# First attention's projection of the tile behind, placed later in the step on every engine, and a second place for the normalised output

## The reference

```python
x = _layernorm(x + _L0_attn_ref(x, Wq, Wk, Wv, proj_w, proj_b))        # 16 heads of 64, causal
x = _layernorm(x + _L0_xattn_ref(x, ctx_1024, ctx_1024, mask, ...))    # 16 heads of 16, context of 77 rows
x = _layernorm(x + _L0_ffn_ref(x, Wr, W1, b1, W2, b2, fw1, ...))       # 8 experts, top 2, capacity, fallback
```

## Time and profile before

| | value |
|---|---|
| Median of three runs | 1508.05 us |
| Time of the profiled execution | 1509.21 us |
| Its span | 1507.5 us |
| PE busy | 1301.3 us (86%) |
| PEld busy | 1079.2 us (72%) |
| DVE busy | 1083.8 us (72%) |
| ACT busy | 924.1 us (61%) |
| POOL busy | 721.1 us (48%) |
| Mean granted clock of PE | 0.956 |
| First and last copy of `o_t` (L782) | 78.8 and 981.3 us, 32 of them |

### The profile page before, as it was taken

How to read it: one execution, slowest core, us unless ns; L and a number is a source line. 1 busy time by engine, 2 the same in 40 slices (tenths; PEclk the granted TensorE clock), 3 DMA queues, 4 the chain that set the end, 5 groups by cost and what they waited for, 6 DMA issues and landing times. The chain is left out here.

```text
span 1507.5 us, 47409 instructions
## 1 busy us (share of the span) xinstructions
PE 1301.3 (86%) x16821; PEld 1079.2 (72%) x16821; DVE 1083.8 (72%) x3112; ACT 924.1 (61%) x2287; POOL 721.1 (48%) x970
## 2 busy tenths in 40 slices
PE   3589999999999999999999999864899999999930
PEld 2478778778878877887887887632688888888820
DVE  4678888888888888888888888748455555555537
ACT  3566777778777777777877766514344444444426
POOL 3144564674565566566556644420243344343326
PEclk9899999999999999999999999995899999999975
DMA  9657767667657667676676664019333363333235
GB/s 222 145 138 161 171 169 160 137 145 175 142 140 184 132 140 190 130 150 155 154 154 142 153 105 90 24 61 421 125 75 76 75 163 93 80 75 77 70 139 206
DMA packets 293216, 208.95 MB, mean 139 GB/s; under 512 B 218782, under 2 KB 250654, under 8 KB 290560
## 3 DMA queue, kind: packets, MB, share of 16 engines
q1 hardware_dynamic: 281952, 184.01, 51.0%
q0 software_dynamic: 6816, 17.71, 4.1%
q10 hardware_dynamic: 4224, 4.19, 0.8%
HBM read 93.79 MB, written 65.93 MB: 106 GB/s over the span
## 5 line engine op out<-in xcount | busy, mean ns | idle before, releaser
L1729 PE MATMUL ps_e<-xt,wres 128*128 128x128 f16 x3408 | 343.5, 220 | 5.2 <-DMA xt<-xg 4.2
L1729 PEld LDWEIGHTS ps_e<-xt,wres 128*128 x3408 | 285.8, 99 | 77.1 <-issue 5.9
L1793 ACT ACTIVATE act_g<-ps_e,b 128x128 f32<-128x128 f32 x568 | 162.4, 369 | 208.1 <-PE ps_e L1729 206.3
L1736 PE MATMUL ps_e<-wres,g_hi 128*128 x568 | 214.5, 379 | 0.8 <-DVE g_lo L1816 0.8
L743 ACT ACTIVATE probs<-st_k,nmax 128x128 f32<-128x128 f32 (+1 forms) x512 | 199.9, 448 | 1.9 <-DVE nmax L964 1.6
L964 DVE CUSTOM_DVE_ANT_0 st_k<-ps,causal 128x128 f32<-128x128 f32 (+1 forms) x512 | 160.6, 351 | 38.0 <-PE ps L444 37.9
L1696 POOL DMA_INDIRECT z_scr<-e_y,dst_i x71 | 82.9, 1168 | 212.6 <-DVE e_y L1807 212.6
L750 ACT ACTIVATE pt_hi<-ps 128x384 f16<-128x384 f32 x256 | 125.2, 489 | 56.0 <-PE ps L452 27.7
L1738 PE MATMUL ps_e<-wres,g_lo 128*128 x568 | 154.8, 273 | 0.0
L452 PE MATMUL ps<-ident,probs 128*128 128x128 f32 x768 | 130.5, 279 | 24.4 <-ACT probs L743 19.3
L969 DVE TENSOR_TENSOR pt_lo<-ps,pt_hi 128x384 f16<-128x384 f32 x256 | 141.4, 552 | 6.0 <-ACT pt_hi L750 2.6
(11 more groups left out here) (281 smaller groups left out, 4044.9 us busy)
## 6 DMA issues: line engine op xcount, KB each, us to landing
k_pair<-k_pair SPq DMA_DIRECT2D x96, 256.0 KB, 6.6
st_p<-in_moe_w SPq DMA_DIRECT2D x24, 768.0 KB, 5.8
w_scr<-st_p SPq DMA_DIRECT2D x24, 768.0 KB, 4.1
wres<-w_scr SPq DMA_DIRECT2D x18, 1024.0 KB, 20.9
v_scr<-v_tok SPq DMA_DIRECT2D x32, 512.0 KB, 4.2
v_pos<-v_scr SPq DMA_DIRECT2D x64, 256.0 KB, 6.1
q_st<-st_q SPq DMA_DIRECT2D x64, 128.0 KB, 2.8
z_scr<-zero SPq DMA_DIRECT2D x32, 256.0 KB, 3.3
```

The source lines that it names most:

```text
L1729: last = mm(out, w(c * FF + f * P, b, P), xt[:, t % X_BUFS, a, c], start=(m == 0), stop=(m == 5))
L1736: mm(out[:, 0:2 * D], g_hi[:, t % G_BUFS, f], w(KC * FF + f * D, 0, 2 * D), start=(f == 0), stop=False, skip_group_check=True)
L1793: nc.scalar.activation(act_g[:, k % 2, f], ps[:, 3 + 2 * (k % 2) + f // 4, (f % 4) * P:(f % 4 + 1) * P], ACT.Gelu, bias=bias[:, f:f + 1], ...
```

## The change

Three engines' `step` functions are rewritten in the same stretch, and one buffer gets a second place.

- On PE, `pv(s, 0)`, `stage_d(s - 2, 1)`, `scores(s, 4)` and `turn_probs(s, 1)` come ahead of the projection `stage_c(s - 1, 1)`, and `fill(s + 1, 4)` directly behind it. The two `value_rows` stand around the second projection `stage_d(s - 2, 2)`.
- On ACT, `stage_c(s - 1, 1)` (only the context's halves, for even tiles) goes behind `pt(s, 1)`, so that `piece` and `stage_d(s - 2, 1)` are ahead of it, and `hi(s + 1, 4)` comes ahead of both `value_rows`.
- On DVE, `y1` with its statistics and moments goes behind `pt(s, 1)`. `lo(s + 1, 4)` follows directly, then the second projection's `y2` with statistics and moments, and only then `first_norm`.
- `o_norm` has two places, used in turn by pairs; DVE's wait on POOL reaches back to the pair before last.

SP's and POOL's orders stay as they are. The diff:

```diff
--- before.py
+++ after.py
@@ -138,7 +138,7 @@
     rden = sb("rden", [P, 4], F32)
     pt_hi = sb("pt_hi", [P, 2, 384], F16)
     pt_lo = sb("pt_lo", [P, 2, 384], F16)
-    o_norm = sb("o_norm", [P, 4, HS], F32)
+    o_norm = sb("o_norm", [P, 2, 4, HS], F32)
     o_st = sb("o_st", [P, 2, 2 * GROUPS, 2, HS], F16)
     o_t = sb("o_t", [P, P, H], F16)
     x_bias = sb("x_bias", [P, D], F32)
@@ -619,23 +619,22 @@
                 pv2(s - 2, 1)
             if has(s):
                 scores(s, 3)
+                pv(s, 0)
+            if has(s - 2):
+                stage_d(s - 2, 1)
+            if has(s):
+                scores(s, 4)
+                turn_probs(s, 1)
             if has(s - 1):
                 stage_c(s - 1, 1)
-            if has(s):
-                pv(s, 0)
+            if has(s + 1):
+                fill(s + 1, 4)
             if has(s - 1):
                 value_rows(s - 1, 0)
             if has(s - 2):
-                stage_d(s - 2, 1)
-            if has(s):
-                scores(s, 4)
-                turn_probs(s, 1)
+                stage_d(s - 2, 2)
             if has(s - 1):
                 value_rows(s - 1, 1)
-            if has(s + 1):
-                fill(s + 1, 4)
-            if has(s - 2):
-                stage_d(s - 2, 2)
             if has(s):
                 turn_probs(s, 2)
             if has(s - 1):
@@ -755,7 +754,7 @@
             act.wait_ge(s_o_norm, pair + 1)
             if g == 1 and since(t, 2):
                 act.wait_ge(s_ot, 2 * (t - 1))
-            nc.scalar.activation(o_st[:, p, 2 * (g - 1):2 * (g + 1), 0], o_norm[:], ACT.Copy).then_inc(s_o_hi, 1)
+            nc.scalar.activation(o_st[:, p, 2 * (g - 1):2 * (g + 1), 0], o_norm[:, pair % 2], ACT.Copy).then_inc(s_o_hi, 1)
 
         def exp2(t, cc):
             act.wait_ge(s_shift, 2 * t + cc + 1)
@@ -832,12 +831,8 @@
                 stage_c(s - 1, 0)
             if has(s):
                 exps(s, 2)
-            if has(s - 1):
-                stage_c(s - 1, 1)
             if 0 <= s - 4 < PIECES:
                 piece(s - 4)
-            if has(s - 1):
-                value_rows(s - 1, 0)
             if has(s - 2):
                 stage_d(s - 2, 1)
             if has(s):
@@ -845,9 +840,12 @@
                 if s == 0:
                     late_split(1)
             if has(s - 1):
-                value_rows(s - 1, 1)
+                stage_c(s - 1, 1)
             if has(s + 1):
                 hi(s + 1, 4)
+            if has(s - 1):
+                value_rows(s - 1, 0)
+                value_rows(s - 1, 1)
             if has(s - 1):
                 stage_c(s - 1, 2)
             if has(s):
@@ -974,9 +972,9 @@
             dve.wait_ge(s_pv, 2 * pair + 2)
             nc.vector.reciprocal(rden[:], o[:, :, 0]).then_inc(s_rden, 1)
             dve.wait_ge(s_rden, pair + 1)
-            if since(t, 1) or g > 1:
-                dve.wait_ge(s_o_lo, pair)
-            nc.vector.tensor_tensor(o_norm[:], o[:, :, 1:1 + HS],
+            if since(t, 1) or g > 3:
+                dve.wait_ge(s_o_lo, pair - 1)
+            nc.vector.tensor_tensor(o_norm[:, pair % 2], o[:, :, 1:1 + HS],
                                     rden[:].unsqueeze(2).to_broadcast([P, 4, HS]), ALU.mult).then_inc(s_o_norm, 1)
 
 
@@ -1079,10 +1077,6 @@
                 pt(s, 0)
                 if s == 0:
                     late_split(0)
-            if has(s - 1):
-                stage_c(s - 1, 1)
-                stats_of(s - 1, 0, y1, s_y1, s_ln1)
-                moments(s - 1, 0, s_ln1, s_mv1)
             if has(s - 2):
                 stage_d(s - 2, 1)
             if has(s):
@@ -1091,15 +1085,18 @@
                 if s == 0:
                     late_split(1)
             if has(s - 1):
-                first_norm(s - 1)
+                stage_c(s - 1, 1)
+                stats_of(s - 1, 0, y1, s_y1, s_ln1)
+                moments(s - 1, 0, s_ln1, s_mv1)
+            if has(s + 1):
+                lo(s + 1, 4)
             if has(s - 2):
                 stage_d(s - 2, 2)
                 stats_of(s - 2, 1, y2, s_y2, s_ln2)
                 moments(s - 2, 1, s_ln2, s_mv2)
             if has(s - 1):
+                first_norm(s - 1)
                 stage_c(s - 1, 2)
-            if has(s + 1):
-                lo(s + 1, 4)
             if has(s - 2):
                 second_norm(s - 2)
             if has(s):
@@ -1268,7 +1265,7 @@
             pair = 4 * t + g // 2
             at = o_st[:, p, 2 * (g - 1):2 * (g + 1)]
             pool.wait_ge(s_o_hi, pair + 1)
-            nc.gpsimd.tensor_tensor(at[:, :, 1], o_norm[:], at[:, :, 0], ALU.subtract).then_inc(s_o_lo, 1)
+            nc.gpsimd.tensor_tensor(at[:, :, 1], o_norm[:, pair % 2], at[:, :, 0], ALU.subtract).then_inc(s_o_lo, 1)
 
         def split_x2(t):
             p = t % 2
```

## The result

The changed kernel takes 1659.88 us, median of 4 runs (1658.79 to 1661.51), against 1508.05: ratio 1.1007 with the interval 1.0988 to 1.1026. It is 10% slower. The forecast was 1625 with a range of 1565 to 1665, so sign and range held, and the value was 35 us too low.

What follows compares the result with a forecast made beforehand. PE was taken as the tighter chain, busy 837.80 of 902.50 us, ahead of DVE. 31 × (3.97 − 0.84) = 97 us plus 20 for the clock on 1509.2 gave 1626, or 1625 against the median; range 1565 to 1665.

Steps and rivals of the forecast that it cites:

- `pv(0)` meets the wait that the projection hid: On PE, pv(0) directly behind scores(3) waits 2.42 us for pt_lo; the old 0.33 us wait goes.
- The delay of `y`: DVE's y starts at mark (pt_lo of group 0 written) + 4.96 us odd, 6.04 even steps: 3.33 and 3.40 later.
- `lo(4)` and the second projection's layer norm ahead of `first_norm`: This DVE order starts PE's L513 about 4.1 us behind y, another 0.8 (odd) and 0.4 us (even) later.
- the delay until L513: Loss per step up to PE's transposes of x1: 4.1 us odd, 3.8 even, 3.97 on average.
- ACT's weight piece, POOL and SP at no cost: ACT's weight copies ahead of stage_c(1) don't delay the projection; POOL's order, SP's transfers unmoved: no cost, 0.6 us without cover.
- Two places for `o_norm` give back 0.84 us a step: DVE's 24.3 us of waits for POOL at L979 go, taken at 0.84 us a step.
- My lower bound of 0.3: Least give-back of o_norm's two places, us a step, from the 9.4 us seen on PE; upper bound 2.1.
- The clock, in 12 of 31 steps: PE's long waits bring 3.4 us at half clock, costing 1.7 us each: 20 us in all.
- the one with the clock falling in every step (1659): Rival: half-clock stretches in every step, 97 us of order and 53 of clock; 20 in 100.
- PE's waits behind L513 (1567): Rival: PE's present idle time of 2.1 us a step closes there, no clock loss, 58 us slower; 14 in 100.
- That DVE's waits of 1.6 to 2.1 us would be filled (1489): Rival: other work fills DVE's waits for the projection, PE's and o_norm's waits go, 20 us faster; 3 in 100.

Runs made afterwards that it cites:

- experiment 3: Kernel before the change with only pv(0) put ahead of the projection on PE: 1599.38 us, ratio 1.0605.
- experiment 6: Changed kernel with DVE's first_norm directly behind y1's moments and lo(4) after it: 1614.12 us, ratio 1.0704.
- experiment 5: Changed kernel with nine matmuls of 512 columns, result unused, between scores(3) and pv(0) on PE: 1617.93 us, ratio 1.0737.
- experiment 1: Kernel before the change with only the two places for o_norm: 1506.06 us, ratio 0.9987.
- Experiments 1 and 2: The second of these: changed kernel with one place for o_norm again, 1661.7 us, ratio 1.1007; the first is experiment 1.
- experiment 4: Changed kernel with PE's projection back directly behind scores(3), ACT's and DVE's orders as changed: 1585.42 us, ratio 1.0505.

## Why the prediction was right, and where its sizes were off

The forecast's sum was 97 us of order and 20 us of clock. Measured: 108.5 and 40.1 in the steps, 1.0 outside them. The medians are 151.8 us apart, 2.2 more than the two profiled executions.

- *`pv(0)` meets the wait that the projection hid.* Right: 2.42 us forecast, 2.32 in the trace's bracket, which counts from the end of the last matmul; from `scores(3)` to the mark, as the forecast counted, with 0.11 for the last matmul again (589.56 + 0.11), it is 592.09 − 589.67 = 2.42. And experiment 3 shows the swap alone costs 2.1 to 2.2 us a step.
- *The delay of `y`.* Right: mark + 4.96 and 6.04 forecast, 4.94 and 6.03 measured. DVE waits for it still, 75.4 us in 29 steps.
- *`lo(4)` and the second projection's layer norm ahead of `first_norm`.* Right: 4.1 us to L513 forecast, 4.02 measured, and experiment 6 takes 1.5 of it away in odd steps. In even ones it regains less, as `k_bd` and `st_xv` are there. Together the delay until L513 is 4.03 us (odd) and 3.74 (even), forecast 4.1 and 3.8. PE stands 1.74 and 0.91 us there, forecast 2.0 and 1.2.
- *ACT's weight piece, POOL and SP at no cost.* Right until L513: in the changed kernel `first_norm` takes 0.38 us in step 15 too, clear of `k_bd`. In experiment 5, steps 2, 3 and 28 to 30, which have no piece, put `y` at mark + 4.95 and 6.03 as well, so the piece had cover. Behind L513 it isn't so clear. There step 29, without a piece, takes 22.54 us and a clean step with one 23.20, and experiment 1 shows POOL without idle time for 12 us ahead of the last `sm_shift`, which ACT and then PE wait for. The prediction did not look there.
- *Two places for `o_norm` give back 0.84 us a step.* **The first failed term.** Experiments 1 and 2 put it at 0.1 us or less. From L513 to the next mark, a clean step of the changed kernel takes 23.20 us, 0.20 less than before; with one place it takes 23.20 too, so these 0.20 are the order's. Over all 31 steps the give-back is 3.89 − 3.50 = 0.39 us. I took DVE's 24.3 us of waits at full value; of them 9.4 reached PE, and even these turned into waits for the exponentials behind, which POOL's list released. My lower bound of 0.3 held, my value was too high, by 0.84 − 0.39 = 0.45 us a step: 14 us. The delay until L513, 0.08 high, gives 2.5 back, hence 11.5 us too little.
- *The clock, in 12 of 31 steps.* **The second failed term**, by 20 us. The mechanism was right and experiment 5 shows it: the clock fell 26 times in 31 steps, and a stretch costs 1.65 us (33.8 us a step where clean ones are 32.2), as 1.7 was forecast. The stretches start (at 83.0, 117.1, 151.2 us and so on) between 0.3 us before and 1.5 us behind a mark, so they belong to the wait of 2.3 us and not to the one before L513. The two waits of the earlier trace rows gave one in two, which was no basis for a share of 12 in 31. Steps 8, 9, 10, 16 and 24 have the same wait and no stretch behind it; what decides between them is not shown.

Of the rivals, the one with the clock falling in every step (1659) has the time to a microsecond, and the reason by three quarters: 26 steps cost 40 of its 53 us, and the smaller give-back made up the rest. PE's waits behind L513 (1567) did not give back 2.1 us a step, but 0.4. That DVE's waits of 1.6 to 2.1 us would be filled (1489) fell by experiment 4: with PE's projection in its old place the new lists of ACT and DVE cost 77 us.

## What to carry to other kernels

Before a long product is moved, ask what it covers. Here 3.7 us of matmuls stood where PE would otherwise have had to wait for a chain of 2.9 us on another engine, and the price of taking them away could be read to a tenth of a microsecond as the distance from PE's last work to the end of that chain. A wait that shows on an engine with slack (DVE's 54.0 us for `y`) is no place for work that waits longer itself. And a second buffer is worth what the *next* wait on the bounding engine leaves of it, which here stood at the end of the step, behind POOL's list, and not at the wait that went.

## What the runs showed of the hardware

- Waits of 2.3 us, once a step, in an otherwise dense stream of matmuls brought 3.4 us at 1.2 GHz 26 times in 31 steps, at the end of the wait or just behind it. Filling them with matmuls whose result nobody reads, which left 0.38 us, was worth 42 us. The same wait brought such a stretch 14 times in experiment 3 and 14 times in experiment 6. Waits of 1.74 us in front of L513 in the changed kernel and in experiment 5 were followed by none, but those of 1.88 us there in experiment 4 by six in fifteen steps. Why a wait brings it in one step and not in the next is not shown.
- The same DVE instruction can take twice as long beside one of POOL: `first_norm`, 128x256 of fp32, takes 0.38 to 0.41 us alone and 0.80 us beside POOL's `k_bd` (experiment 6).
- A wait put down to "issue" in a weight-load row need not be one of its own. In the kernel before these took 20.0 us in front of L470, 45 of them: one of 0.25 us in each step, and one of 0.77 in every other step, which stands just ahead of a matmul that waits for `o_norm`. Step 15, timelines of PEld and PE:

```profile
507.71 0.10 PEld L470 LDWEIGHTS ps<-v_pos,pt_hi 128*128 128x128 f16 x1 [0.77 <-issue]
507.74 0.19 PE L470 MATMUL ps<-v_pos,pt_hi 128*128 128x65 f16 x1 [0.56 <-DVE o_norm L979]
```

  With two places both waits are gone, and 8.4 us in 30 waits are left. What releases the ones of 0.25 us is not shown by any run here.
